# Six filler matmuls ahead of the channel mix, behind the sum of the time mix

## The reference

```
x = layernorm(x + time_and_channel_mix(x))      # "L0_attn"
x = layernorm(x + soft_tree(x))                 # "L0_ffn", 8 levels, 256 leaves
x = layernorm(x + causal_attention(x))          # "L1_attn", 16 heads of 8, rotary
x = layernorm(x + experts(x))                   # "L1_ffn", 16 experts, best 2, and 2 shared
```

```
x   = ln(x, ln0); xn = ln(x, pre)
k   = exp(min(mix(xn, k) @ tm_Wk, 60)); v = mix(xn, v) @ tm_Wv; r = mix(xn, r) @ tm_Wr
wk, wkv = two decaying sums over the tokens of k and of k * v
x   = x + (sigmoid(r) * wkv / (wk + 1e-8)) @ tm_Wo        # time mix; this sum is x2
xn  = ln(x, post)
kv  = silu(mix(xn, cm_k) @ cm_Wk) @ cm_Wv                 # channel mix
x   = x + sigmoid(mix(xn, cm_r) @ cm_Wr) + kv             # y0
```

## Time and profile before

| | |
|---|---|
| median of 3 runs | 1983.46 us (1978.99 to 1986.34) |
| the profiled execution | 1981.15 us |
| its span, first to last instruction | 1979.4 us |
| mean granted TensorE clock | 0.944 of full speed |
| TensorE busy | 1664.5 us, 84% |
| VectorE busy | 1526.5 us, 77% |
| ScalarE busy | 1005.9 us, 51% |
| GpSimd busy | 914.3 us, 46% |

### The profile page before, as it was taken

The page is one execution under the profiler, slowest core; times in us unless marked ns, Lnnn a source line. Parts: engine busy times, 40 slices in busy tenths (PEclk is TensorE's granted clock), DMA queues, the critical chain, the costliest instruction groups (busy, mean ns, idle before and its releaser), DMA issues.

```text
span 1979.4 us, 33699 instructions
## 1 busy us (share of the span) xinstructions
PE 1664.5 (84%) x12063; PEld 1082.8 (55%) x12141; DVE 1526.5 (77%) x3386; ACT 1005.9 (51%) x1997; POOL 914.3 (46%) x1117
## 2 busy tenths in 40 slices
PE   1365799989898999989898989989898989988785
PEld 1133456565565656565565656565665657564535
DVE  2756879889797979889797979789797969783712
ACT  1232374655646374655556474746556464736252
POOL 3436253635545363635455364636355463622202
PEclk9677899999999999999999999999999999999887
DMA  3001010010101010010101010100101010100000
GB/s 97 0 6 48 7 39 17 8 54 8 54 8 49 7 54 6 24 37 8 54 7 49 7 54 7 37 25 8 54 8 54 2 54 2 45 11 25 31 7 6
DMA packets 64617, 53.35 MB, mean 27 GB/s; under 512 B 6018, under 2 KB 63170, under 8 KB 64450
## 3 DMA queue, kind: packets, MB, share of 16 engines
q1 hardware_dynamic: 64450, 51.19, 8.4%
HBM read 8.44 MB, written 4.19 MB: 6 GB/s over the span
## 4 chain that ended last, share of the span: by engine, by line
PE 42%; DVE 36%; issue 6%; ACT 5%; SPq 5%; POOL 3%; DMA 3%; DVEq 0%; ACTq 0%; POOLq 0%
PE bank L871 40%; DVE rmax L742 12%; SPq L300 4%; DVE rmax L739 3%; DVE wkb L689 3%; ACT prob L463 3%; DVE prob L822 3%; PE bank L867 3%; DMA kh<-part 2%; DVE stats L643 2%; DVE tree L652 1%; DVE kvsum L681 1%; DVE kk L665 1%; SPq L312 1%; DVE ksum L676 1%
## 5 line engine op out<-in xcount | busy, mean ns | idle before, releaser
L463 ACT ACTIVATE prob<-bank 128x512 f32<-128x512 f32 x640 | 359.4, 600 | 85.6 <-PE bank L871 80.1
L742 DVE TENSOR_REDUCE rmax<-bank 128x1 f32<-128x512 f32 (+2 forms) x768 | 353.4, 504 | 29.6 <-PE bank L871 29.1
L871 PE MATMUL bank<-kh,qh 72*128 72x512 bf16 (+3 forms) x1024 | 259.8, 308 | 52.8 <-DVE rmax L742 38.1
L871 PE MATMUL bank<-qh,kh 75*128 75x512 bf16 (+3 forms) x1024 | 257.4, 306 | 24.7 <-ACT prob L463 20.8
L871 PE MATMUL bank<-wexpT,prob 128*128 128x128 f32 x2048 | 271.7, 280 | 2.1 <-POOL prob L429 0.6
L871 PEld LDWEIGHTS bank<-wexpT,prob 128*128 128x128 f32 x2048 | 258.7, 195 | 21.0 <-issue 15.9
L429 POOL TENSOR_TENSOR prob<-xdT,spread 128x512 f32<-128x512 f32 x128 | 173.6, 1356 | 193.5 <-ACT spread L463 193.4
L463 ACT ACTIVATE spread<-bank 128x512 f32<-128x512 f32 x128 | 76.5, 597 | 298.1 <-PE bank L871 251.1
L871 PEld LDWEIGHTS bank<-qh,kh 75*128 75x128 bf16 x1024 | 100.1, 98 | 205.4 <-ACT prob L463 146.0
L689 DVE RECIPROCAL wkb<-wkb 128x512 f32<-128x512 f32 x64 | 211.6, 3326 | 0.0
L871 PE MATMUL bank<-maskb,identb 128*128 128x128 bf16 x1024 | 194.3, 223 | 0.0
(11 more groups left out here) (209 smaller groups left out, 3401.6 us busy)
## 6 DMA issues: line engine op xcount, KB each, us to landing
qh<-part SPq DMA_DIRECT2D x144, 128.0 KB
kh<-part SPq DMA_DIRECT2D x144, 128.0 KB
x<-in_L_attn_x_dram SPq DMA_DIRECT2D x16, 256.0 KB, 2.9
out_dram<-yo SPq DMA_DIRECT2D x16, 256.0 KB, 2.3
qh<-maxT SPq DMA_DIRECT2D x16, 48.0 KB
wk<-in_L_attn_tm_Wk_dram SPq DMA_DIRECT2D x1, 256.0 KB
wv<-in_L_attn_tm_Wv_dram SPq DMA_DIRECT2D x1, 256.0 KB
wr<-in_L_attn_tm_Wr_dram SPq DMA_DIRECT2D x1, 256.0 KB
```

The source lines that it names most:

```text
L463: raised(act.activation(dst, src, func, **kw), signal)
L742: last = dve.tensor_reduce(rmax[:, j, h:h + 1], S[n % 2][:, col:col + (j + 1) * P], AX_X, ALU.max)
L871: return pe.matmul(out_, w, x, start=start, stop=stop, **kw)
```

## The change

A step `busy_channel` is added, and three of them are put into TensorE's order, between `3:attn_out` and `1:cmk0`. Each waits for `x2` of its batch and calls `keep_busy(T1)`, that is two bf16 matmuls of 128x128 by 128x512. Six matmuls a batch, 96 in all. `cmk0` starts a new sum in T1, so their result isn't read. The other tokens of the table are the same and in the same order.

```diff
-        3:back1 3:attT 1:xn2T 3:attn_out 1:cmk0 1:cmk1 3:xdT 2:row0 2:row1 3:centroids 1:cmk2 2:row2 2:row3 1:cmk3 2:row4 2:row5 1:cmr 2:row6 1:cmv0
...
+        3:back1 3:attT 1:xn2T 3:attn_out 1:busy_channel0 1:busy_channel1 1:busy_channel2 1:cmk0 1:cmk1 3:xdT 2:row0 2:row1 3:centroids 1:cmk2 2:row2
...
+            def busy_channel(b, k):
+                until(pe, b, "x2")
+                keep_busy(T1)
+
...
-                **each("busy_in", 3, busy_in), **each("busy_post", 3, busy_post), **each("busy_tree", 3, busy_tree),
+                **each("busy_in", 3, busy_in), **each("busy_post", 3, busy_post), **each("busy_tree", 3, busy_tree), **each("busy_channel", 3, busy_channel),
```

More of the change, by code:

```diff
@@ L83 @@
         3:score36 3:back0 3:score37 3:score38 3:score39 1:read_out0 1:read_out1 1:read_out2 1:read_out3 3:weigh12 3:weigh13 3:weigh14 3:weigh15 2:attn_v
-        3:back1 3:attT 1:xn2T 3:attn_out 1:cmk0 1:cmk1 3:xdT 2:row0 2:row1 3:centroids 1:cmk2 2:row2 2:row3 1:cmk3 2:row4 2:row5 1:cmr 2:row6 1:cmv0
[L85 to L89, removed]
+        3:back1 3:attT 1:xn2T 3:attn_out 1:busy_channel0 1:busy_channel1 1:busy_channel2 1:cmk0 1:cmk1 3:xdT 2:row0 2:row1 3:centroids 1:cmk2 2:row2
+        2:row3 1:cmk3 2:row4 2:row5 1:cmr 2:row6 1:cmv0 1:cmv1 1:cmv2 1:cmv3 2:row7 2:row8 3:shared 2:row9 2:row10 3:gT 0:xnT 2:row11 2:row12 3:gb0
+        3:biases 3:gb1 3:expert0 3:gb2 2:row13 2:row14 3:gb3 3:expert1 1:xbT 2:row15 2:row16 3:gb4 0:k0 2:row17 3:expert2 0:v0 2:row18 2:row19 0:r0 3:gb5
+        3:expert3 2:row20 2:row21 3:gb6 3:expert4 2:row22 1:gates0 2:row23 3:gb7 2:row24 1:gates1 0:v1 2:row25 2:row26 3:expert5 2:row27 3:gb8 2:row28
+        0:k1 3:expert6 2:row29 2:row30 3:gb9 3:expert7 2:row31 2:row32 3:gb10 0:r1 3:expert8 2:row33 3:gb11 2:row34 3:expert9 2:row35 3:gb12 2:row36
+        3:expert10 2:row37 3:gb13 2:row38 3:gb14 2:row39 3:expert11 3:gb15 0:k2 2:maxT 3:expert12
     """,
```

## The result

| | before | changed |
|---|---|---|
| median, 8 runs each | 1982.43 us (1978.69 to 1986.34) | 1972.88 us (1966.20 to 1975.99) |
| ratio, 95% interval | | 0.9949 (0.9933 to 0.9966) |
| profiled execution, its span | 1981.15, 1979.4 us | 1972.05, 1970.2 us |
| mean granted clock | 0.944 | 0.956 |

The change saves 9.6 us of the median (about 7 to 13), where 4.2 was forecast. The direction was right, but the forecast gain is less than half of the measured one, and the time lies just under the low end of the range.

A forecast was written before the change was run, and what follows sets the result against it. No single engine was taken to bound it: TensorE and VectorE hold 42% and 36% of the chain. Terms -2.06 + 0.84 - 3.0 = -4.2 us; against the median 1983.46 that is 1979.3, given as 1979 us, range 1973 to 1988.

The forecast's parts named there:

- The gap, its cause and the cost of the fillers: Before `cmk0`: 2.74 us idle waiting for `mix3`; fillers leave 1.4 us, `cmk0` isn't late, extra cost taken as 0.
- The clock: At `cmk0` and `cmk1`: it falls to 1.2 GHz after the gap; filled, the block takes 1.98 us, not 3.30.
- The rule of the Trainium skill: Warns only of longer idle gaps; by it the clock would not fall before `cmk0`, and time would stay at 1983.
- Filling, 3.0 us: Batches 0 and 1, while the pipeline fills: channel mix 1.5 us sooner each; lower end 0, upper 4.3.
- Steady turns, -2.06 + 0.84 = -1.2 us: The 14 full-pipeline turns: 2.06 us gained where transfers are in time, 0.84 lost to one moved slow stretch.
- -2.06: Four 1.2 GHz turns with transfers in time give back 0.69 + 0.49 + 0.41 + 0.47 us against 3.27.
- +0.84 for a stretch that moves behind `row0`: In turns set by transfers, one of two turns gains a 1.2 GHz stretch in the scores, costing 0.84 us.
- rival 2: Slower: the low-clock stretch moves behind `row0` in transfer-set turns, +1.3 to +4.6 us, 1985 to 1988; chance 0.13.
- The floor of 3.27 us: `row0` starts 3.27 us after `cmk0` at 2.4 GHz with transfers in time, since `xdT` waits 0.79 us for ScalarE.
- The seven waits: Seven turns where `row0` starts as the transfers land: seven waits, 7.2 us; the four at 1.2 GHz gain nothing.
- The range: Whole time 1973 to 1988 us: lowest run with the larger gain, to the upper end of rival 2.
- the larger gain: Rival 3: turns 0.5 us shorter, batch 0 at 2.4 GHz throughout, no stretch moves; -6.4 us, 1977; chance 0.12.

The follow-up runs named there:

- e4: Changed kernel with all 96 fillers 16 columns wide instead of 512; 1980.70 us, ratio 0.9989 to the kernel before.
- e14: Kernel before with qh/kh transfers cut to half their columns from batch 1 on, and fillers in batches 0 and 1 only; 1966.57 us, ratio 0.9928.
- e7: Kernel before, no fillers, with the 18 qh/kh transfers cut to half their columns from batch 1 on; 1970.96 us, ratio 0.9946.
- e1: The kernel before once more, no edit, for a second trace; 1982.02 us, ratio 0.9992.
- e2: Changed kernel with the fillers in batches 0 and 1 only; 1976.93 us, ratio 0.9974 to the kernel before.
- e3: Changed kernel with the fillers in batches 2 to 15 only; 1974.94 us, ratio 0.9948 to the kernel before.
- e12: The changed kernel once more, no edit, for a second trace; 1974.88 us, ratio 0.9953 to the kernel before.
- e8: Changed kernel, six fillers a batch, with qh/kh transfers cut to half their columns from batch 1 on; 1959.74 us, ratio 0.9889 to the kernel before.
- e15: Kernel before with qh/kh transfers cut to half their columns from batch 1 on, and fillers in batches 2 to 15 only; 1963.99 us, ratio 0.9904.
- e6: Changed kernel with two more fillers between cmk1 and xdT and two between xdT and row0; 1972.42 us, ratio 0.9942 to the kernel before.
- e9: Changed kernel with the nine kh transfers issued by ScalarE, the nine qh by SyncE; 2060.02 us, ratio 1.0388 to the kernel before.
- e13: Changed kernel with four of the 18 transfers (kh) issued by ScalarE, 14 by SyncE; 1967.13 us, ratio 0.9923 to the kernel before.

## Why the prediction was half right

- **The gap, its cause and the cost of the fillers: right.** 1.44 us of idle time is left ahead of `cmk0`, which follows `mix3` as before; nothing is late.
- **The clock: right, and shown.** No block of the steady turns is at 1.2 GHz in any of ten traces with six fillers or more from batch 2 on, against 6 to 12 of 14 in six traces without. e4 shows that the work in the fillers does it, not their presence. The rule of the Trainium skill that the prediction weighed (TensorE: Matmul & The Clock Gate, "HAM oscillation — how this bites in real kernels") falls for this place: the clock does fall behind gaps of 2.74 us, and filling them keeps it up.
- **Filling, 3.0 us: right.** 2.7 to 3.4 by the traces, 4.4 by e14.
- **Steady turns, -2.06 + 0.84 = -1.2 us: this is the step that failed.** The runs give 3.4 to 5.7 us. Both terms were mis-sized.
  - **-2.06 should have been about -4.4** (2.0 to 6.4 in the four traces without fillers and with whole transfers). The sum was read off one execution, and where the clock falls against the block comes out differently in every execution: the block is low in 8, 8, 12, 8, 9 and 6 turns of 14 in the six traces that have no filler there or none that works. The price of a plain low turn was right: 0.41 to 0.69 us by the prediction, 0.36 to 0.71 in e7. But the trace of before had the fewest us lost in turns in time, and it lacks two kinds that the others have: a stretch of 6.8 us over block and first scores (2.4 to 2.5 us; e1, e2, e7), and one that begins 5.4 to 5.6 us behind `cmk0` with nothing late (1.2 us; e1, e4, e7, e14).
  - **+0.84 for a stretch that moves behind `row0` was not owed.** Stretches that begin 4 us or more behind `cmk0` number 5, 3, 2 and 4 in the traces without (before, e1, e2, e4) and 3, 3 and 2 with (changed, e3, e12), and late turns cost no more with fillers than without: no more are made that these traces can tell. That the late turns gain nothing from the faster block was right for seven of ten such turns, and what the other three lose isn't explained. The mechanism of rival 2 is real (4.8 us in the turn at 512.40), but it isn't the change's. Its price was read low, too: 1.0 to 1.3 us where 0.84 was taken, because the first 0.35 us by which `row0` is late cost nothing.
- **The turn of batch 15: put at nothing.** In the trace of before its block was at 2.4 GHz, so nothing was expected of it, though it can pay as any other, and its loss would lie behind the 13 distances. From the last `cmk0` to the end e7 takes 242.9 us and e8 239.0, but e14 and e15 242.1 and 243.1. So some 2 us of the 11.2 aren't placed: chance of the drain, or batch 15.
- **The floor of 3.27 us: right as a floor, wrong as a price list.** `row0` starts 3.27 or 3.28 us behind `cmk0` in every turn from batch 3 on of the changed kernel that has its transfers in time. But e6, with `row0` at 3.70 and a turn only 0.05 us longer, shows that `row0`'s start doesn't carry the loss of a low block: a turn of e7 with `row0` at 3.69 and a low block is 0.36 over. That the prices read off `row0` came out right is in part luck; by what path the block delays the turn was not tried.
- **The seven waits.** The 7.2 us of the earlier trace rows aren't the seven turns: six waits are in turns, the seventh lies in the drain, and in the seventh turn (batch 2) `row0` starts 0.05 us behind the landing without a wait. The sum doesn't use them.
- **The range** held the larger gain only as batch 0 at 2.4 GHz throughout; it should have had a larger steady term, which the scatter between executions would have told.

## What to carry to other kernels

Work that nothing reads, put into a gap of the matmul engine that is set by another engine, can keep the clock up at no cost that shows; here it fitted the gap, and with ten matmuls instead of six, too long for the gap of the first two batches at the lower clock, nothing was lost either. When a loss depends on where something falls by chance, don't sum it over the turns of one trace: take the price of each kind of turn and its frequency, and leave room for kinds that the trace doesn't show. To measure a gain of half a per cent under a scatter of the same size, take a source of the scatter out of both kernels (here: shorter transfers), and compare the steady parts of their traces turn by turn; the whole times of those kernels still differ by 6 to 11 us from run to run. And when a change seems to bring something forward, say against what it was timed: in e9 the transfers came ahead of `cmk0` only because `cmk0` was late.

## What the runs showed that I had not expected

- Operands of which most are zero can hold the clock: `bias_rows` is zero but for three of its 128 rows (`ones_rows` is all ones), and with it the granted clock stays at 1.00 through the block in all steady turns. The width of the matmul counts: with 16 columns the block is low in 8 of 14 turns, as without fillers. Other operands were not tried.
- 18 transfers whose issues begin at the same time in every turn (the last score is always 13.8 us ahead of `cmk0`) land 1.7 to 6.4 us behind `cmk0`. Half their size lands them within 0.15 us of `cmk0` in most turns, and takes 11 us off the kernel before (e7), about as much as the change does.
- A DMA issue took 0.64 us on SyncE alone, and longer on both engines when ScalarE issued beside it: 0.98 on SyncE and 1.07 on ScalarE with nine each, 0.77 and 0.87 with 14 and four. The transfers landed 0.4 to 0.7 us earlier in the mean by it, not the 2.6 (e13) or up to 5.9 (e9) that were expected of the earlier issues.
- A gap can drop the clock for 6.8 us instead of 3.4, in the same place, at four to five times the price (2.4 us against 0.56).
- `row0` may be up to 0.35 us late for nothing; beyond that a late transfer is paid one for one.
